# Random features: the sum of the key features over a chunk's four token tiles moves to GpSimd

## The reference, cut to what matters

```
phiQ = favorplus_features(Q, proj) * inv_sqrt_m
phiK = favorplus_features(K, proj) * inv_sqrt_m
KV = jnp.einsum('bhtm,bhtd->bhmd', phiK, V)
Ksum = jnp.sum(phiK, axis=2)
num = jnp.einsum('bhtm,bhmd->bhtd', phiQ, KV)
den = jnp.einsum('bhtm,bhm->bht', phiQ, Ksum)[..., None] + EPS
out_heads = num / den
```

## Time and profile before

| what | us |
|---|---|
| median of 3 runs | 1217.03 (1211.1, 1217.03, 1218.83) |
| the profiled execution | 1211.25 |
| its span on the core | 1208.9 |
| TensorE matmul busy | 1102.3 (91%) |
| VectorE busy | 931.1 (77%) |
| ScalarE busy | 812.0 (67%) |
| GpSimd busy | 234.9 (19%) |

### The profile page before, as it was taken

How to read it: one execution, slowest core, us unless ns; L and a number is a source line. 1 busy time by engine, 2 the same in 40 slices (tenths; PEclk the granted TensorE clock), 3 DMA queues, 4 the chain that set the end, 5 groups by cost and what they waited for, 6 DMA issues and landing times.

```text
span 1208.9 us, 20220 instructions
## 1 busy us (share of the span) xinstructions
PE 1102.3 (91%) x7428; PEld 614.3 (51%) x7436; DVE 931.1 (77%) x1521; ACT 812.0 (67%) x1292; POOL 234.9 (19%) x332
## 2 busy tenths in 40 slices
PE   7978899999999989989999899898888888898987
PEld 3333344444444445467765354466666666463354
DVE  5997798777777677767775578699999896576966
ACT  6885655555555654755576646888888776868774
POOL 1000000000000001200000013487878776000000
PEclk9999999999999999989999999899999998999999
DMA  6000112121221000000000000000000000000002
GB/s 177 1 0 1 56 56 67 65 62 61 62 61 61 27 1 0 10 1 2 2 1 1 1 0 9 1 3 2 2 3 2 16 2 2 9 1 1 1 1 69
DMA packets 26361, 27.17 MB, mean 22 GB/s; under 512 B 4171, under 2 KB 17308, under 8 KB 26268
## 3 DMA queue, kind: packets, MB, share of 16 engines
q1 hardware_dynamic: 25936, 25.91, 7.3%
q10 hardware_dynamic: 332, 0.01, 0.0%
HBM read 23.30 MB, written 2.62 MB: 21 GB/s over the span
## 4 chain that ended last, share of the span: by engine, by line
PE 61%; DVE 19%; ACT 12%; issue 6%; POOL 1%; DMA 0%; ACTq 0%; DVEq 0%
PE psum L723 9%; PE psum L734 9%; PE psum L726 4%; PE psum L87 4%; PE psum L983 4%; PE psum L955 3%; PE psum L1634 2%; PE psum L1965 2%; DVE arena L2151 2%; PE psum L1382 2%; DVE N L2160 2%; ACT ln_std L114 2%; ACT ln_std L116 2%; PE psum L105 1%; ACT N L2065 1%
## 5 line engine op out<-in xcount | busy, mean ns | idle before, releaser
L762 ACT ACTIVATE arena<-psum 128x512 f32<-128x512 f32 x128 | 69.5, 594 | 114.5 <-PE psum L723 114.5
L723 PE MATMUL psum<-arena,weights 128*128 128x512 f32 x256 | 122.2, 600 | 1.7 <-DVE N L128 1.0
L734 PE MATMUL psum<-arena,weights 128*128 128x512 f32 x256 | 120.3, 592 | 0.0
L620 DVE SCALAR_TENSOR_TENSOR arena<-diff,vecs,N 128x512 f32<-128x512 f32 x128 | 95.1, 745 | 0.0
L682 DVE SCALAR_TENSOR_TENSOR arena<-arena,psum 128x512 f32<-128x512 f32 x64 | 43.9, 686 | 62.8 <-PE psum L734 62.8
L2065 ACT ACTIVATE N<-N 128x1024 f32<-128x1024 f32 x64 | 67.8, 1059 | 32.2 <-DVE N L2160 31.6
L1975 PE MATMUL psum<-ident,N 128*128 128x128 f32 x512 | 73.0, 288 | 13.3 <-POOL N L2120 12.7
L723 PEld LDWEIGHTS psum<-arena,weights 128*128 128x128 f32 x256 | 48.2, 191 | 62.4 <-issue 57.9
L734 PEld LDWEIGHTS psum<-arena,weights 128*128 128x128 f32 x256 | 48.6, 190 | 61.4 <-issue 61.4
L1965 PE MATMUL psum<-arena 32*128 32x128 f32 x1024 | 77.2, 290 | 1.6 <-ACT arena L2043 1.4
L2061 ACT ACTIVATE arena<-psum 128x1024 f32<-128x1024 f32 x64 | 65.6, 1024 | 19.2 <-PE psum L1975 19.0
(11 more groups left out here) (330 smaller groups left out, 2491.0 us busy)
## 6 DMA issues: line engine op xcount, KB each, us to landing
arena<-tw_rows SPq DMA_DIRECT2D x64, 256.0 KB, 3.1
out_dram<-arena SPq DMA_DIRECT2D x8, 256.0 KB, 3.6
arena<-in_L_attn_a_x_dram SPq DMA_DIRECT2D x3, 512.0 KB, 6.7
weights<-in_L_attn_a_eWk_dram SPq DMA_DIRECT2D x1, 1024.0 KB, 6.0
arena<-in_L_attn_a_x_dram SPq DMA_DIRECT2D x2, 256.0 KB, 3.9
weights<-in_L_attn_a_eWr_dram SPq DMA_DIRECT2D x1, 512.0 KB, 9.9
tw_rows<-arena SPq DMA_DIRECT2D x2, 128.0 KB, 2.7
tw_rows<-arena SPq DMA_DIRECT2D x1, 256.0 KB, 3.5
```

Of the source, the lines that this page charges most:

```text
L620: op = nc.vector.scalar_tensor_tensor(mixed[:, n % 4, a, :], k.diff[:, q % 2, :], k.vec((f"cm_k{e}", f"cm_r{e}")[a]), before, ALU.mult, AL ...
L723: op = nc.tensor.matmul(k.bank[2 * (n % 2) + h][:], k.eWk[:, e, h * P:(h + 1) * P], mixed[:, n % 4, 0, :], start=True, stop=True)
L734: op = nc.tensor.matmul(k.bank[4 + n % 2][:], k.eWv[:, e, h, :], ks[:, (2 * (n % 2) + h) * CH:(2 * (n % 2) + h + 1) * CH], start=(h == 0), ...
L762: op = nc.scalar.activation(kr[:, h * CH:(h + 1) * CH], k.bank[2 * (n % 2) + h][:], ACT.Relu)
```

## The change

TensorE's products with ones are taken out of the loop over token tiles. GpSimd adds the four token tiles of a half, in two additions (128x512 into `pairs`, 128x256 into `tokens`), and TensorE multiplies the result with ones once for a chunk, in the gather of its second half. A semaphore `fv_tokens` orders it. A chunk has 4 products with ones where it had 16.

```diff
+    pairs, tokens = part(CH), [part(CH) for _ in range(2)]
...
-                for part in range(2):
-                    for g in range(G):
-                        w = k.fv_ones if part else va[c % 2][:, t * P + g * 32:t * P + (g + 1) * 32]
-                        op = nc.tensor.matmul(to[32 * g:32 * (g + 1), part * P:(part + 1) * P], w,
-                                              ex[(2 * c + g // 2) % 5][:, g % 2 * CH + t * P:g % 2 * CH + (t + 1) * P],
-                                              start=(n % 4 == 0 and j == 0 and part == 0), stop=(n % 4 == 3 and j == 1 and part == 1), skip_group_check=True)
+                for g in range(G):
+                    op = nc.tensor.matmul(to[32 * g:32 * (g + 1), 0:P], va[c % 2][:, t * P + g * 32:t * P + (g + 1) * 32],
+                                          ex[(2 * c + g // 2) % 5][:, g % 2 * CH + t * P:g % 2 * CH + (t + 1) * P],
+                                          start=(n % 4 == 0 and j == 0), stop=False, skip_group_check=True)
+            if n % 2 == 1:
+                pe.wait_ge(k.fv_tokens, 4 * c + 4)
+                for g in range(G):
+                    op = nc.tensor.matmul(to[32 * g:32 * (g + 1), P:2 * P], k.fv_ones, tokens[c % 2][:, g * P:(g + 1) * P],
+                                          start=False, stop=(n % 4 == 3), skip_group_check=True)
...
+    @block.gpsimd
+    def _(pool):
+        for n in range(HALF):
+            c = n // 2
+            by_token = ex[n % 5].rearrange("p (g t m) -> p g t m", g=2, t=4)
+            halves = pairs.rearrange("p (g t m) -> p g t m", g=2, t=2)
+            pool.wait_ge(k.fv_exp, n + 1)
+            if n >= 1:
+                pool.wait_ge(k.fv_tokens, 2 * n)
+            nc.gpsimd.tensor_tensor(halves, by_token[:, :, 0:2], by_token[:, :, 2:4], ALU.add).then_inc(k.fv_tokens, 1)
+            pool.wait_ge(k.fv_tokens, 2 * n + 1)
+            if c >= 2:
+                pool.wait_ge(k.fv_used, 2 * c - 2)
+            nc.gpsimd.tensor_tensor(tokens[c % 2].rearrange("p (g m) -> p g m", g=G)[:, n % 2 * 2:n % 2 * 2 + 2],
+                                    halves[:, :, 0], halves[:, :, 1], ALU.add).then_inc(k.fv_tokens, 1)
```

More of the change, by code:

```diff
@@ L2293 @@
               "fv_score", "fv_max", "fv_off", "fv_arg", "fv_exp", "fv_used", "fv_ysum", "fv_acc", "fv_sums", "fv_kv",
-              "fv_exT", "fv_ratio", "fv_ln", "fv_rd", "fv_o", "fv_out", "fv_x"]
+              "fv_exT", "fv_ratio", "fv_ln", "fv_rd", "fv_o", "fv_out", "fv_x", "fv_tokens"]
 SEGMENT_SEMS = ["sw_in", "sw_mask", "sg_proj", "sg_first", "sg_kv", "sg_q", "sg_kd", "sg_vd", "sg_score", "sg_max", "sg_arg", "sg_exp",
@@ L2453, in build @@
          k.fv_score, k.fv_max, k.fv_off, k.fv_arg, k.fv_exp, k.fv_used, k.fv_ysum, k.fv_acc, k.fv_sums, k.fv_kv,
-         k.fv_exT, k.fv_ratio, k.fv_ln, k.fv_rd, k.fv_o, k.fv_out, k.fv_x) = (ctx.enter_context(nc.semaphore(name)) for name in FAVOR_SEMS)
+         k.fv_exT, k.fv_ratio, k.fv_ln, k.fv_rd, k.fv_o, k.fv_out, k.fv_x, k.fv_tokens) = (ctx.enter_context(nc.semaphore(name)) for name in FAVOR_SEMS)
         (k.passed, k.ln1_in, k.ident_zero, k.ident_one, k.consts_set, k.vrows_set, k.vecs_in, k.vecs_turned,
```

## The result

The changed kernel takes 1229.61 us (median of 4 runs, 1228.43 to 1232.94) against 1217.28 us before (4 runs beside it); the ratio is 1.0109 with a 95% interval of 1.0079 to 1.0139. It is slower, by about 12 us, where I had forecast +1.35 us and a range up to 1225.

What follows compares the result with a forecast made beforehand. VectorE and ScalarE were taken to bound the keys' part, TensorE a close second. TensorE's relief of -0.45 us and VectorE's hold of +1.8 summed to +1.35 us, about 1218 us, with 8 in 10 between 1210 and 1225.

Steps and rivals of the forecast that it cites:

- who holds `scores` of an odd half: Keys' part: scores(9) starts only after the statistics of half 8, its weight load idle 0.76 us for VectorE's L1795.
- pair one: Halves 8 and 9 of the keys' part: 7.80 us of VectorE and one `scores`, with no gather between.
- The odd gather's saving: Odd halves' gathers: 0.21 us less work each, about nothing left after a new wait taken at 0.20 us.
- term for the relief: TensorE's removed products: 0.35 us gained at the start and 0.1 behind the last gather, together -0.45 us.
- The phase, and with it the hold: Keys' part: L1791 held by running GpSimd additions, 0.45 us a period, 1.8 us over four; ends 0 and 3.0.
- E: End of exp n in the keys' part; GpSimd reads from E + 0.08 to 0.92 and E + 1.21 to 1.73.
- The clock: Rival: TensorE's gaps lower the granted clock, 2 to 5 falls of up to 1.4 us, +3 to +7; chance 0.14.
- The rival with VectorE held in every half: Keys' part: each L1791 loses about 1.0 us to GpSimd, sixteen halves make 16 us, 1233 us; chance 0.05.
- the held VectorE with the worst of the clock: Whole kernel: the case for being slower by over 1%; chance 0.06.
- the period: Sign: four halves of the keys' part take 15.3 to 16.1 us; below 15 would prove the forecast wrong.
- the longest norms' addition: Sign: L1791's longest row in the profile after is 0.4 to 0.8 us, its median above 0.19.
- the clock fell in the middle of the keys: Sign of being wrong: the granted clock falling midway through the keys' part.

Runs made afterwards that it cites:

- e1: Changed kernel without GpSimd's additions or the wait for them; the 4 products with ones a chunk read only the first token tile: 1222.57 us, ratio 1.0032.
- e7: Kernel before, no GpSimd, with products with ones of each odd gather moved into the even gather ahead of it: 1217.17 us, ratio 0.9996.
- e8: e3 plus 12 products with ones that nobody reads in each even gather: 1216.93 us, ratio 0.9985 to the kernel before.
- e2: Kernel before plus GpSimd's 32 additions, at once and unread, TensorE's work as before: 1221.79 us, ratio 1.0038.
- e3: Changed kernel, with GpSimd's additions also waiting until the norms' addition of the next half is done: 1222.74 us, ratio 1.0044 to the kernel before.
- e6: Changed kernel, additions at once, with the norms' addition replaced by a VectorE instruction with one SBUF input: 1223.36 us, ratio 1.004 to the kernel before.
- e5: Kernel before plus GpSimd's 32 unread additions, begun only after the norms' addition of the next half: 1218.5 us, ratio 1.0004.
- e11: Kernel before, no GpSimd, without the products with ones of the odd gathers (token tiles 2 and 3): 1219.22 us, ratio 1.001.
- e15: e9 again, one profiled run: 1224.52 us.
- e10: Kernel before, no GpSimd, without the products with ones of the even gathers (token tiles 0 and 1): 1224.86 us, ratio 1.0046.
- e4: Changed kernel again, no edit: 1230.42 us, ratio 1.0105 to the kernel before.
- e12 to e14: Three more profiled runs of the kernel before, no edit: 1215.24, 1217.02 and 1218.95 us.
- e9: Changed kernel, additions at once, plus 12 products with ones that nobody reads in each even gather: 1226.68 us, ratio 1.0084 to the kernel before.

## Why the prediction was wrong

**The step that failed first: who holds `scores` of an odd half.** I wrote that "only then does `scores(9)` start", because its weight load is idle 0.76 us "<-DVE L1795", and concluded that no gather lies on the path of pair one. But the code waits there for `fv_arg` of half s - 2, as the section on the kernel before has it: half 7, long done. The idle time is that of the weight loads behind the long `project`, and in half 17, where the subtraction L1795 of the half ahead runs on until 587.35, the trace of before has the same row with another releaser:

```profile
586.59 0.97 PEld L1634 LDWEIGHTS psum<-weights,arena 32*128 32x128 f32 x16 [0.76 <-issue]
```

TensorE's own queue (`scores(8)`, gather, `values`, `project`) was the bound of pair one. So its relief did bring the odd statistics forward: in e1 `scores(9)` starts at 560.11, before the subtraction of half 8 ends (559.15 + 1.23 = 560.38), where in the kernel before it started 0.1 us behind its end. e7 shows what that is worth: 0.43 us less in an odd gather bring the odd statistics 0.44 us forward and take 0.25 us off a period. The odd gather's saving, which I had put at "about nothing" against a wait of 0.20 us, was there too: from the gather of half 5 to `values` it is 0.79 us in the changed kernel (558.35 to 559.14) and was 1.01 us (553.90 to 554.91), so the new wait cost nothing. My term for the relief was -0.45 us; in e8, without holds or new falls of the clock, the keys' part is 1.0 us shorter.

**The phase, and with it the hold.** The mechanism was right, and so was the condition. Its size was a term mis-sized: I had L1791 of half 9 at E + 1.51, in GpSimd's second addition, for 0.22 us. It came at E + 0.38 (563.56 against 562.12 + 1.06 = 563.18), at the start of the first addition, for 0.81 us. Of these 1.13 us of phase 0.41 are the earlier maximum of half 9 (3.64 us behind that of half 8, where it was 4.05), and 0.72 come from half 8, whose own hold made exp 8, and with it E, later. Half 8 was held for 0.73 us where I had 0, for two reasons. Its addition of the norms came at E + 0.46, not E + 0.98, as its maximum stands 3.03 us behind that of half 7 instead of 3.52; and the first GpSimd addition takes 1.27 us, not the 1.05 that I took from the segment stage. That row is a product with one input broadcast (L2119), and the 1.22 of L886 a product of a tile with itself, so neither priced this addition; I had 1.22 as an upper bound for the sum of GpSimd's work, and didn't carry it into the phases. The relief of TensorE and the hold of VectorE thus weren't two terms to add: the one moved the phase of the other. But the hold was too small in my sum without that: in e2, where TensorE isn't relieved, it is 4.5 us in the rows against my 1.8, since each hold moves the phase of the next half. I had weighed the phase for the timing of before alone. Of the measured cost e3 shows 7 to 8 us, where I had 1.8 and an upper end of 3.0.

**The clock.** I gave it 0.14 and +3 to +7 us for 2 to 5 falls. It costs 3.7 to 3.8 us, net of what the relief gives back (e1 and e3; e6 agrees with them within 1 us), and 5.8 us between e3 and e8, both within the range that I gave it, but it wasn't an unlikely case. My argument against it, that gaps of 0.3 us a period had not let the clock fall, held only for the gap of before, and there not always: in e7's profile the clock fell once behind a wait of 0.30 us (549 to 553 us). e1 has 1.14 us and the changed kernel 1.85 us. Where I said "a shorter gather lets TensorE wait longer at the same point", I had the cause in hand and costed it at nothing.

**The rival with VectorE held in every half** (0.05, 16 us) had a price of 1.0 us a hold, and the holds were near it (rows of 0.92 to 1.27 us, less 0.19), but seven came, not sixteen. It and the clock together make the result, which I had only as "the held VectorE with the worst of the clock", at 0.06.

**What was right.** 320 records for the gathers' matmuls (770 in the keys' part instead of 961), GpSimd no bound, the wait for the sum satisfied, L1804, L1815 and L1832 unchanged beside GpSimd. Of the other signs, the period (16.9 us, outside 15.3 to 16.1) and the longest norms' addition (1.27 us, over 0.8) missed, and the clock fell in the middle of the keys, which I had named as a sign of being wrong. The Trainium skill's rule ("SBUF — State Buffer", Who interferes with whom), that a VectorE instruction with two SBUF inputs waits for a GpSimd one that reads SBUF, and one with a single input doesn't, is borne out on both sides by e6, e3 and e5. By its letter the hold lasts until the other has finished; in the two rows above it ends 0.14 to 0.15 us before the end of GpSimd's row, if the addition's own 0.19 is taken off (I had 0.21 from the earlier trace rows).

**Open.** Segment stages of the four profiles of before are 241.5 to 246.4 us, those of e1 to e11 and e15, but for e7 and e10, 246.4 to 249.9, and that of after 250.6. e5, whose total is that of before, has 247.4, so most of this is spread of the clock. Outside the keys' part there is more to explain: e4's keys' part is 8.5 us longer than that of e12 to e14 (80.2 against 71.7), its total 11.5 us longer than that of the kernel before. Whether these 3 us follow from the moment at which a stage begins isn't settled, and e9's surplus is in the same place. Nothing was run that shifts the start of the segment stage alone. Additions at once, against late ones, cost 3.3 us with TensorE as before (e2, e5), 7 to 8 us with it thinned and 9.7 us with it filled (e9, e8), while the holds in the rows are 4.5, 5.9 and 4.9 us: so the hold's price isn't its length, and how much of it comes through the clock isn't taken apart. Nor is it shown whether the clock follows the work left out or the length of the wait, since the filling of e8 mends both. Length alone doesn't decide: the clock fell behind waits of 0.55 us in e15 and not behind one of 0.55 in e9, and behind one of the three waits of 0.74 us in e11.

## What to carry to other kernels

A wait that the profile puts down to another engine must be held against the code before it is believed: the same idle time with "issue" a few halves on told that the queue itself was the bound. When a step frees one engine, redo the phases of all that run beside it, since an instruction that used to miss a GpSimd row may now meet it: the VectorE addition with two SBUF inputs and the GpSimd additions wanted an order between them, and one wait (e3) gave 7 us. Take the price of an instruction from one of the same operation and operands: the product with a broadcast input had 1.05 us, the addition 1.27. And where TensorE's clock fell behind its waits, as here, work taken out of a place where it waits anyway wasn't free; e8 was 5.8 us faster for doing products that nobody reads.

## What the runs showed of the hardware

In the profiles of e1 and of the changed kernel the granted clock fell to 1.2 GHz in each period from half 4 on, at or within 3 us behind TensorE's wait (0.95 to 1.54 us in e1, 1.85 to 2.27 us in the changed kernel), and stayed there about 7 us in e1, and about 4 or 7 us in the changed kernel. A GpSimd addition of 128x512 with both inputs from one tile of this stage takes 1.26 to 1.31 us, and one of 128x256 0.72 to 0.73; the product of 128x512 with one input broadcast takes 1.04 to 1.06 us in the segment stage (L2119). Neither e7 nor e8 can be told from the kernel before, so no faster version came out of this.
